# Carry add of a scan step: from GpSimd to a one-column ScalarE activation, with the other work placed anew

## The reference

```python
# feed-forward (f0 before, f1 after the Mamba block), on the layer-normed rows
xr = mu_r * x + (1 - mu_r) * x_prev          # x_prev: the token before
xk = mu_k * x + (1 - mu_k) * x_prev
r = sigmoid(xr @ W_r); k_act = square(relu(xk @ W_k))
x = x + 0.5 * (r * (k_act @ W_v))
# Mamba, on the layer-normed rows
xs, z = split(xn @ W_in.T)                   # 1024 channels each
xc = silu(b_conv + 4-tap causal convolution of xs)
dt_low, B, C = split(xc @ W_xproj.T)         # 32, 16 and 16 columns
delta = softplus(dt_low @ W_dt.T + b_dt)
h[t] = exp(delta * A) * h[t-1] + delta * B[t] * xc     # 16 states per channel
y = sum over states of h * C + D_skip * xc
x = x + (y * silu(z)) @ W_out.T
```

## Time and profile before

| | |
|---|---|
| median of three runs | 4893.23 us (4893.09 to 4894.3) |
| profiled execution, first to last instruction | 4888.0 us (the page gives the span alone; 5.2 us less than the median) |
| first scan starts; scans of chunks 1 to 15 start | 153.6; every 291 to 293 us from 442.0 on |
| last chunk's scan ends | 4782.1 us |
| DVE, PE, POOL, ACT busy in the span | 92%, 88%, 65%, 59% |

### The profile page before, as it was taken

How to read it: one execution, slowest core, us unless ns; L and a number is a source line. 1 busy time by engine, 2 the same in 40 slices (tenths; PEclk the granted TensorE clock), 3 DMA queues, 4 the chain that set the end, 5 groups by cost and what they waited for, 6 DMA issues and landing times.

```text
span 4888.0 us, 58099 instructions
## 1 busy us (share of the span) xinstructions
PE 4296.9 (88%) x16896; PEld 2382.9 (49%) x16896; DVE 4488.3 (92%) x3650; ACT 2900.1 (59%) x6355; POOL 3196.4 (65%) x3328
## 2 busy tenths in 40 slices
PE   6777989898999989989898899989999898999787
PEld 2444545454554545545454454545545454554443
DVE  2799999999999999999999999999999999999992
ACT  2555656666666566656666665666656666665452
POOL 1666767576676767767576676767667576776770
PEclk9888999999999999999999999999999999999798
DMA  2445555454554555555555554555555565655451
GB/s 82 141 135 180 172 171 185 163 183 162 189 169 151 189 168 186 172 173 185 158 174 163 186 172 152 190 179 176 172 185 173 155 180 156 190 170 153 167 164 62
DMA packets 423053, 810.71 MB, mean 166 GB/s; under 512 B 41264, under 2 KB 41264, under 8 KB 418640
## 3 DMA queue, kind: packets, MB, share of 16 engines
q1 hardware_dynamic: 422736, 807.00, 52.1%
HBM read 772.25 MB, written 34.60 MB: 165 GB/s over the span
## 4 chain that ended last, share of the span: by engine, by line
DVE 38%; PE 29%; issue 16%; ACT 7%; POOL 6%; DMA 3%; DVEq 0%; SPq 0%; POOLq 0%; ACTq 0%
DVE decay L1091 19%; DVE g L1099 10%; PE y_acc L567 6%; PE mm L494 5%; PE mm L483 5%; POOL dbx L1298 4%; PE mm L472 4%; DVE xc L1037 3%; DMA c_all<-bc_scratch 2%; PE mm L531 2%; PE mm L509 2%; PE mm L519 2%; DVE xc L1043 1%; ACT decay L889 1%; POOL xout L1287 1%
## 5 line engine op out<-in xcount | busy, mean ns | idle before, releaser
L1298 POOL TENSOR_TENSOR dbx<-u,b_all 128x1024 f32<-128x1024 f32 x1024 | 2414.2, 2358 | 902.6 <-DVE g L1099 901.7
L1091 DVE TENSOR_TENSOR_SCAN decay<-decay,state,dbx 128x1024 f32<-128x1024 f32 x1024 | 2405.4, 2349 | 172.4 <-ACT decay L889 157.6
L567 PE MATMUL y_acc<-ident,g 128*128 128x128 f32 x8192 | 1124.2, 283 | 372.5 <-DVE g L1099 370.6
L567 PEld LDWEIGHTS y_acc<-ident,g 128*128 128x128 f32 x8192 | 947.4, 144 | 939.1 <-DVE g L1099 713.2
L1099 DVE TENSOR_TENSOR g<-decay,c_all 128x1024 f32<-128x1024 f32 x1024 | 1244.3, 1215 | 10.0 <-DMA c_all<-bc_scratch 1.1
L886 ACT ACTIVATE decay<-delta,neg_a 128x512 f32<-128x512 f32 x1024 | 708.7, 692 | 36.9
L889 ACT ACTIVATE decay<-delta,neg_a 128x511 f32<-128x511 f32 x1024 | 686.9, 671 | 0.0
L895 ACT ACTIVATE state<-decay 128x2 f32<-128x2 f32 x1024 | 166.9, 163 | 508.6 <-DVE g L1099 506.1
L494 PE MATMUL mm<-wbuf_c,col 128*128 128x512 f32 x1024 | 460.9, 594 | 2.1 <-ACT col L758 1.3
L1037 DVE SCALAR_TENSOR_TENSOR xc<-mm,conv_sb,xc 128x509 f32<-128x509 f32 (+2 forms) x384 | 285.3, 743 | 47.0 <-ACT xs_last L804 35.7
L1302 POOL TENSOR_TENSOR dbx<-dbx,carry 128x1 f32<-128x1 f32 x1024 | 274.2, 268 | 80.3
(11 more groups left out here) (100 smaller groups left out, 5107.4 us busy)
## 6 DMA issues: line engine op xcount, KB each, us to landing
b_all<-bc_scratch SPq DMA_DIRECT2D x1024, 256.0 KB, 3.4
c_all<-bc_scratch SPq DMA_DIRECT2D x1024, 256.0 KB, 3.6
wbuf_d<-in_w_r SPq DMA_DIRECT2D x32, 1024.0 KB, 7.5
wbuf_c<-in_w_v SPq DMA_DIRECT2D x32, 1024.0 KB, 7.3
xin<-in_x SPq DMA_DIRECT2D x16, 1024.0 KB, 6.8
wbuf_c<-in_w_k SPq DMA_DIRECT2D x16, 1024.0 KB, 6.7
wbuf_d<-in_w_in SPq DMA_DIRECT2D x16, 1024.0 KB, 5.8
wbuf_a<-in_w_in SPq DMA_DIRECT2D x16, 1024.0 KB, 8.0
```

The lines of the kernel that those rows point to most:

```text
L567: last = pe.matmul(y_acc[:, tb, j * P:(j + 1) * P], g[:, s % PAIRS, j, tb * P:(tb + 1) * P], ident[:, :], start=n == 0 and j == 0 and tb % ...
L1091: dve.tensor_tensor_scan(d, d, flat(dbx[:, s % DBX, :, :]), state[:, batch, s, 0:1], ALU.mult, ALU.add).then_inc(scan_done, 1)
L1298: pool.tensor_tensor(dbx[:, s % DBX, :, :], u[:, q % 2, :, :], b_all[:, s % BRING, :].unsqueeze(1).broadcast_to([P, QT, W]), ALU.mult).the ...
```

## The change

The add at L1302 goes from POOL's queue. In its place `make_decay` on ACT gets an activation (Identity, the carry as its bias, one column) between the save and the Exp; it waits for `dbx_done` of its own step. `dbx_done` now counts one per step and not two, `decay_done` four and not three, and the scan no longer waits for `dbx_done` itself. The product of a quarter's first step waits for `u` alone; ACT waits for the carry. The new `pool_weigh` and `POOL_WEIGH` are empty and issue nothing. Nearly every table of steps has other numbers, and `ZEROS` has one zero matmul where there were eight.

```diff
-        XPROJ = (49, 50)
-        ZEROS = {2: 2, 31: 2, 39: 2, 30: 1, 53: 1}
+        XPROJ = (48, 49)
+        POOL_WEIGH = ()
+        POOL_WEIGH_AT = ()
+        ZEROS = {31: 1}
...
-                    sp.wait_ge(dbx_done, 2 * count)
+                    sp.wait_ge(dbx_done, count)
...
                 if n == 0:
                     act.wait_ge(h_act.sem, h_act.at(it, f"xb{q}"))
+                    act.wait_ge(h_pool.sem, h_pool.at(it, f"carry{q}"))
+                act.wait_ge(dbx_done, NSTEP * it + s + 1)
+                first = dbx[:, s % DBX, 1, 0:1]
+                act.activation(first, first, ACT.Identity, bias=carry[:, q % 2, n:n + 1]).then_inc(decay_done, 1)
...
             def scan(it, s, batch):
-                dve.wait_ge(dbx_done, 2 * (NSTEP * it + s + 1))
...
-                dve.wait_ge(decay_done, 3 * (NSTEP * it + s + 1))
+                dve.wait_ge(decay_done, 4 * (NSTEP * it + s + 1))
...
                 if n == 0:
-                    pool.wait_ge(h_pool.sem, h_pool.at(it, f"carry{q}"))
+                    pool.wait_ge(h_pool.sem, h_pool.at(it, f"u{q}"))
...
-                pool.wait_ge(dbx_done, 2 * (NSTEP * it + s) + 1)
-                pool.tensor_tensor(dbx[:, s % DBX, 1, 0:1], dbx[:, s % DBX, 1, 0:1], carry[:, q % 2, n:n + 1],
-                                   ALU.add).then_inc(dbx_done, 1)
```

More of the change, by code:

```diff
@@ new lines, in build @@
+        YTURN = (31, 31, 39, 39, 62, 62, 66, 66)
+        DT = (-11, 2, 18, 33)
+        SUM_SKIP = (3, 26, 33, 52)
+        OUT = ((3, 4), (19, 20), (21, 22), (23, 23))
+        MM_K = ((5, 6, 7, 8), (46, 47, 49, 51))
+        MM_R = ((9, 11, 11, 13), (40, 41, 44, 44))
+        MM_V = ((14, 15, 16, 17), (54, 54, 55, 56))
+        MTURN = (23, 24, 24, 25)
+        Z = (27, 29, 32, 37, 58, 58, 60, 62)
+        XS = (28, 30, 33, 36, 38, 40, 43, 46)
+        XPROJ = (48, 49)
+        POOL_WEIGH = ()
@@ new lines, in build, with weighed @@
+        BANK = {"f0T": (1, 0, 1, 0), "YT": (0, 0, 1, 1, 0, 1, 1, 0), "dt": (0, 1, 1, 0, 1, 0, 0, 1), "o":
[3 rows of a table added]
+        ON_POOL = [sum(q < s for q in POOL_WEIGH) for s in range(NSTEP + 1)]
+        def weighed(it, s):
+            n = NSTEP * it + s
+            if n < 0:
+                return None
+            it, s = divmod(n, NSTEP)
+            if s in POOL_WEIGH:
+                return pool_weighed, ON_POOL[NSTEP] * it + ON_POOL[s] + 1
+            return mult_done, (NSTEP - ON_POOL[NSTEP]) * it + s - ON_POOL[s] + 1
@@ L332, in load_c @@
             def load_c(k, s):
-                if due(count := NSTEP * k + s - CRING + 1):
-                    sp.wait_ge(mult_done, count)
+                if read := weighed(k, s - CRING):
+                    sp.wait_ge(*read)
                     sp.sem_inc(passed_sp, 1)
@@ L828, in softplus @@
                     if due(count := NSTEP * (k - 1) + NS * (q + 3)):
-                        act.wait_ge(decay_done, 3 * count)
+                        act.wait_ge(decay_done, 4 * count)
                     if due(count := h_pool.at(k - 1, f"u{q + 2}")):
@@ L892, in save @@
             def save(it, s, batch):
-                act.wait_ge(mult_done, NSTEP * it + s + 1)
-                act.activation(state[:, batch, s, :], decay[:, s % PAIRS, :, W - 1], ACT.Copy).then_inc(saved, 1)
+                if s in POOL_WEIGH:
+                    act.wait_ge(scan_done, NSTEP * it + s + 1)
+                    h = dbx[:, s % DBX, :, W - 1]
+                else:
+                    act.wait_ge(*weighed(it, s))
+                    h = decay[:, s % PAIRS, :, W - 1]
+                act.activation(state[:, batch, s, :], h, ACT.Copy).then_inc(saved, 1)
             def body(it, bt):
@@ L1088, in scan @@
                         dve.wait_ge(saved, count)
[L1089 to L1091 removed]
+                dve.wait_ge(decay_done, 4 * (NSTEP * it + s + 1))
+                d, v = flat(decay[:, s % PAIRS, :, :]), flat(dbx[:, s % DBX, :, :])
+                dve.tensor_tensor_scan(v if s in POOL_WEIGH else d, d, v, state[:, batch, s, 0:1],
                                        ALU.mult, ALU.add).then_inc(scan_done, 1)
@@ L1159, in body @@
                         row_means(1, f_dve[1], b)
-                    if scn:
+                    if scn and s not in POOL_WEIGH:
                         weigh(it, s)
@@ L1290, in product @@
                 q, n = divmod(s, NS)
-                if due(count := NSTEP * it + s - DBX + 1):
-                    pool.wait_ge(mult_done, count)
+                if read := weighed(it, s - DBX):
+                    pool.wait_ge(*read)
+                    pool.sem_inc(passed_pool, 1)
+                if (s - DBX) % NSTEP in POOL_WEIGH:
+                    pool.wait_ge(saved, NSTEP * it + s - DBX + 1)
                     pool.sem_inc(passed_pool, 1)
                 if n == 0:
-                    pool.wait_ge(h_pool.sem, h_pool.at(it, f"carry{q}"))
+                    pool.wait_ge(h_pool.sem, h_pool.at(it, f"u{q}"))
                     pool.sem_inc(passed_pool, 1)
@@ L1310, in body @@
                         product(it, s)
+                        for n in at(POOL_WEIGH_AT, s):
+                            pool_weigh(it, POOL_WEIGH[n])
                     if scn:
```

82 lines of the change are left out of this document (41 added, 41 removed), and 6 rows, old and new, of the table BANK.

## The result

The changed kernel took 4959.02 us (median of four runs, 4954.08 to 4967.47) against 4893.39: ratio 1.0138, 95% interval 1.0123 to 1.0152. It is slower, by 66 us, where 66 us less was forecast. The profiled execution took 4956.76 us, its span is 4954.9.

The account below looks back on a forecast made before the run. DVE was taken to bound the kernel, with 11.46 us idle a period. Gains of 7.67 and 0.6 less 3.9 of new waits give 4.4 us a period, 66 over fifteen chunks: 4827 us, range 4770 to 4885.

Parts of the forecast that it names:

- step 7: DVE's two mixing instructions took 2.17 us there beside POOL's late product; moving `u` to step 14 should give 0.6 us.
- the rule on the shared port: GpSimd contends with two-SBUF-input VectorE instructions; DVE could gain up to 0.27 us in some 16 steps, left out of the forecast.
- Steps 15 and 52: Scan waits of 3.62 and 4.05 us behind ACT's blocked queue should go wholly, 7.67 us a period.
- New waits: Scan waits added in steps 11, 18, 20, 35, 59 and 60, 3.9 us a period together.
- Step 20: Delta's table load and softplus stay as before; 0.1 us more on a scan wait of 0.90.
- Step 11: The first receptance Tanh, ahead of the decays on ACT, makes the scan 1.2 us late.
- The activation: One-column carry add on ACT: 0.25 us for its operand, 0.1 added delay per step; ACT some 16 us busier a period.
- The clock: Rival, chance 0.13: with one zero matmul, half-clock stretches ahead of the first output product delay step 11; 4852 us.
- the bound of 1.7: Most that one half-clock stretch of 3.4 us at a period's start can hold back products, in us.
- POOL setting the pace in steps 58 to 62: Rival, chance 0.08: ACT's Exps wait for POOL's products, steps last 5.5 us against 4.06; 4933 us.

Follow-up runs that it names:

- zeros_back: The changed kernel with the eight zero matmuls of the kernel before in place of one; 4968.99 us, ratio 1.0166.

## Why the prediction was wrong

The step that failed is the sentence "The change adds no work to DVE and takes none away", and with it the view that idle time alone was at stake, so that the question was only which waits go and which come. DVE's busy time rose by 4.66 us a period, since the profile counts an instruction that waits for the port as busy. The forecast amounts to a period of 287.3 us, 279.6 of them busy and 7.7 idle. The changed kernel has 9.3 us more: 5.1 of busy time and 4.2 of idle time, where the forecast also lacked waits, above all in steps 48, 47 and 11. With the head additions alone put back (`heads_back`) the busy time is 279.61, as forecast, and 2.7 us of idle time remain over it.

The mechanism stood in the prediction, in step 7; I used it for what the move of `u` takes away, and asked of the moved head additions neither what they wait for nor what is late behind them. A row of before pointed at it: the head additions already sat 238.0 us for the taps. Where I weighed the rule on the shared port I priced it by the carry add, 0.27 us, and not by the product of 2.36 us.

Point by point:

- Steps 15 and 52, 7.67 us: right. These scans start without a wait:

```profile
1695.45 2.35 DVE L1115 TENSOR_TENSOR_SCAN decay<-decay,state,dbx 128x1024 f32<-128x1024 f32 x1
...
1875.69 2.35 DVE L1115 TENSOR_TENSOR_SCAN decay<-decay,state,dbx 128x1024 f32<-128x1024 f32 x1
```

- Step 7, 0.6: right; the group `xn_col` went from 1010 to 872 ns, 64 times, 0.6 us in each of 15 chunks. A new wait there, 0.48 us in 6 of 13 periods, takes 0.2 of it back.
- New waits (means over 13 periods): 18, 0.29 against 0.3; 35, 0.54 against 0.7; 59, 1.28 against 1.35; 60, 0.71 against 0.85: right. Step 20 0.84, where 1.0 was forecast. Step 11 is the exception, 2.2 against 1.2.
- Not forecast: 48 with 2.1 us, 47 with 1.0, 62 with 0.6, 37 with 0.4. Step 48's is SP's queue, whose moved loads of weights I didn't follow past the transfers of C; I did it for x alone. Step 47's is the long step 45, behind which TensorE fell to half clock and the last xs product came late.
- The activation took 0.289 us, under the 0.31 beyond which I would have been wrong. ACT's busy time rose by 5.9 us a period (76.1 in thirteen) and not by 16, since most of it lies under its neighbours. ACT's save and Exp in one step before:

```profile
1649.90 0.15 ACT L895 ACTIVATE state<-decay 128x2 f32<-128x2 f32 x1
1650.09 0.69 ACT L886 ACTIVATE decay<-delta,neg_a 128x512 f32<-128x512 f32 x1
```

and after, with the new activation between:

```profile
1667.75 0.15 ACT L920 ACTIVATE state<-decay 128x2 f32<-128x2 f32 x1
1667.80 0.28 ACT L901 ACTIVATE dbx<-dbx,carry 128x1 f32<-128x1 f32 x1
1667.98 0.68 ACT L906 ACTIVATE decay<-delta,neg_a 128x512 f32<-128x512 f32 x1
```

  From the save's start to the Exp's it was 0.19 us and is 0.23: 0.04 in this step (the median over all steps went from 0.20 to 0.25), where 0.1 was taken.
- The clock: the rival had the place right, and its cause, the missing zeros, is not refuted for this place. In step 4, ahead of the first output product, the clock was 0.50 in one period and 1.00 in the next:

```profile
1648.40:1651.70 3.30, 3.30 (x5) 1.35 (x4) 3.30 (x4) 2.28 (x9) 1.49 (x1) 0.50 0.35 125
1944.00:1947.30 3.30, 3.30 (x9) 1.34 (x9) 3.30 (x3) 2.88 (x7) 2.19 (x1) 1.00 0.62 200
```

and the scans of step 11 in these two periods:

```profile
1681.34 2.36 DVE L1115 TENSOR_TENSOR_SCAN decay<-decay,state,dbx 128x1024 f32<-128x1024 f32 x1 [2.86 <-ACT decay L909]
...
1975.94 2.36 DVE L1115 TENSOR_TENSOR_SCAN decay<-decay,state,dbx 128x1024 f32<-128x1024 f32 x1 [1.62 <-ACT decay L909]
```

In all 13 periods the wait is 1.6 us without such a stretch and 2.9 with one (six of them): 1.25 us, below the bound of 1.7. These six periods took 297.6 us on average, the others 295.7, with other half-clock stretches in both. In `zeros_back` the clock fell in step 1 of 12 periods, and in step 4 of none:

```profile
1635.40:1638.80 3.40, 2.97 (x14) 2.57 (x14) 3.37 (x3) 2.96 (x12) 2.23 (x2) 0.50 0.96 299
1648.40:1651.70 3.30, 3.30 (x16) 1.81 (x15) 3.30 (x4) 2.28 (x10) 1.44 (x2) 1.00 0.39 135
```

and step 11 waited 1.6 us in all 13:

```profile
1679.45 2.36 DVE L1115 TENSOR_TENSOR_SCAN decay<-decay,state,dbx 128x1024 f32<-128x1024 f32 x1 [1.60 <-ACT decay L909]
```

  So having one zero in place of eight may have cost 0.6 us a period here; but the eight lost more elsewhere (0.55 us in step 31, 0.8 more in 47), and the whole is a small part of the miss.

- POOL setting the pace in steps 58 to 62: no; of these scans only those of 59 and 60 wait, as in the forecast.

With the head additions and the loads put back, the two things that I had not followed, the kernel takes 4837 us (`loads_back`), where 4827 was forecast. The period there is 288.29 us, 3.5 less than before, against the 4.4 of the forecast.

## What to carry to other kernels

When an instruction is moved up on an engine that runs ahead, look up which step of which other engine makes its operand: it takes the engine's whole lead away, and what it does when it catches up lands somewhere else. On DVE, idle time is no bound on what a change can cost, since an instruction with two SBUF operands that meets POOL's grows inside its busy time; compare means by form, not busy shares. A load moved up in a queue in order is priced by the wait it brings and by the transfers behind it.

## What the hardware showed

Meeting POOL's 2.36-us product made a 0.74-us mixing up to 2.82 us long, and the block runs both ways: the product that began under the first mixing of step 45 took 2.80 us. The 0.9 us that the mixing takes in most steps already holds some 0.2 us of it, since the product begun under the scan ends some 0.36 us after the mixing's start; where no product was in flight the mixing took 0.74.
